# Making the first pair's operands of a feed-forward inside the last attention slots, and reordering a kernel's first loads

## The reference, cut to what matters

```python
x = layernorm(x + autocorrelation_attention(x))   # top lag 0 dominates on these data
sim = softmax(einsum("ncs,nds->ncd", ctx, x) * 256 ** -0.5, axis=1)
x = layernorm(x + einsum("ncd,nds->ncs", sim, ctx))
x = layernorm(x + x @ W_base.T + moe_lora(x, gate_W, A, B))   # 8 experts, rank 8, top 2
```

## Time and profile before

| | |
|---|---|
| three timed runs | 1957.73, 1959.69, 1960.36 us |
| median | 1959.69 us |
| the profiled execution | 1960.41 us |
| its span, first to last instruction | 1958.6 us |
| mean granted TensorE clock | 0.971 of full |
| busy: PE, DVE, ACT, POOL | 1783.3, 1362.4, 792.3, 171.4 us |
| DMA | 472.70 MB, mean 241 GB/s |

### The profile page before, as it was taken

How to read it: one execution, slowest core, us unless ns; L and a number is a source line. 1 busy time by engine, 2 the same in 40 slices (tenths; PEclk the granted TensorE clock), 3 DMA queues, 4 the chain that set the end, 5 groups by cost and what they waited for, 6 DMA issues and landing times. The chain is left out here.

```text
span 1958.6 us, 27039 instructions
## 1 busy us (share of the span) xinstructions
PE 1783.3 (91%) x10210; PEld 952.3 (49%) x10210; DVE 1362.4 (70%) x2607; ACT 792.3 (40%) x939; POOL 171.4 (9%) x362
## 2 busy tenths in 40 slices
PE   3899999999944969999999999998899999999997
PEld 2666666666621434445444445443344444444443
DVE  3888888888859866777666777689655565465553
ACT  5788888888745212222222212133222222122211
POOL 1212121212100000000000000000010010001000
PEclk8999999999976979999999999999999999999999
DMA  8799999999768499999999999955989988988883
GB/s 280 188 292 267 282 257 296 263 289 252 229 197 241 124 233 250 267 251 235 259 258 252 248 231 232 223 167 161 283 249 257 272 235 256 258 259 228 262 251 118
DMA packets 565595, 472.70 MB, mean 241 GB/s; under 512 B 498448, under 2 KB 502544, under 8 KB 544656
## 3 DMA queue, kind: packets, MB, share of 16 engines
q1 hardware_dynamic: 565456, 470.87, 87.7%
HBM read 237.51 MB, written 109.58 MB: 177 GB/s over the span
## 5 line engine op out<-in xcount | busy, mean ns | idle before, releaser
L1585 PE MATMUL bank_f<-w_hi_f,a_cols_f 128*128 128x512 f16 x3584 | 1091.9, 382 | 79.0 <-DMA a_cols_f<-rows_f 58.7
L1585 PE MATMUL bank_f<-w_lo_f,a_cols_f 128*128 128x512 f16 x1792 | 684.4, 382 | 0.0
L1585 PEld LDWEIGHTS bank_f<-w_hi_f,a_cols_f 128*128 128x128 f16 x3584 | 352.5, 98 | 509.3 <-DVE w_lo_f L1312 40.1
L1164 ACT ACTIVATE rows_f<-xn_f 128x1024 f16<-128x1024 f32 x78 | 82.4, 1057 | 497.7 <-DMA xn_f<-x_scratch 339.5
L1585 PEld LDWEIGHTS bank_f<-w_lo_f,a_cols_f 128*128 128x128 f16 x1792 | 176.2, 98 | 204.5 <-issue 4.0
L1343 DVE SCALAR_TENSOR_TENSOR y_f<-bank_f,w_iscale_f,y_f 128x512 f32<-128x512 f32 x192 | 134.6, 743 | 169.2 <-PE bank_f L1585 169.1
L656 PE MATMUL ps_s_fast<-k_both_fast,q_hi_fast 128*128 128x256 f16 x1024 | 171.2, 275 | 8.0 <-DMA k_both_fast<-v_lo_fast 7.0
L1343 DVE SCALAR_TENSOR_TENSOR y_f<-bank_f,w_iscale,y_f 128x512 f32<-128x512 f32 x192 | 134.9, 744 | 45.3 <-PE bank_f L1585 37.3
L1304 DVE TENSOR_TENSOR rows_f<-xn_f,rows_f 128x1024 f16<-128x1024 f32 x78 | 94.4, 1210 | 92.3 <-ACT rows_f L1164 92.3
L1304 DVE TENSOR_TENSOR rows_f<-sums_f,rows_f 128x1024 f16<-128x1024 f32 x63 | 76.9, 1221 | 112.5 <-ACT rows_f L1164 112.4
L1164 ACT ACTIVATE rows_f<-sums_f 128x1024 f16<-128x1024 f32 x63 | 66.3, 1053 | 199.3 <-DMA a_cols_f<-rows_f 196.9
(11 more groups left out here) (215 smaller groups left out, 2288.4 us busy)
## 6 DMA issues: line engine op xcount, KB each, us to landing
xbuf_fast<-x SPq DMA_DIRECT2D x32, 1024.0 KB, 7.9
x_scratch<-x2buf_fast SPq DMA_DIRECT2D x32, 1024.0 KB, 5.5
y_f<-x_scratch SPq DMA_DIRECT2D x32, 1024.0 KB, 8.0
xn_f<-x_scratch SPq DMA_DIRECT2D x62, 512.0 KB, 4.8
kept_scratch<-a_cols_f SPq DMA_DIRECT2D x45, 512.0 KB, 3.4
xn<-x_scratch SPq DMA_DIRECT2D x45, 512.0 KB, 6.7
a_cols_f<-kept_scratch SPq DMA_DIRECT2D x45, 512.0 KB, 9.0
cbuf<-ctx_in SPq DMA_DIRECT2D x16, 1024.0 KB, 5.5
```

What stands on the lines that cost most here:

```text
L1164: nc.scalar.activation(rows[g % 2][:, 0], source(i), ACT.Copy).then_inc(a_hi, 1)
L1585: ins = nc.tensor.matmul(bank[i][:], a_cols[:, i, part + kk, :], ww[:, W_SLOT[i], kk, :], start=(kk == 0 and part == 0 and ww is w_hi), st ...
```

## The change

1. **First loads.** In slot -2 SP issues context 0 and x 0, then the four key transposes of batch 0, with context 1 behind each of the last two, and only then x 1 and the tables. Weight tiles 0 and 1 are loaded for slots 1 and 2 instead of 0 and 1. DVE does both `value_low` of batch 0 before `x_stats(1)`.
2. **Pair 0's items in the attention.** `a_cols` becomes a buffer of the whole program. In the attention, `q_lo`, `q_hi`, the table `inv` and the two halves of x2's second tile live in it, until the items overwrite them. x2's rows 128 to 255 are loaded at the end of slot 12, rows 0 to 127 into `cbuf[0]` in slot 13. In slot 14 POOL makes the five sums and differences (`first_sum`), ACT the seven high parts (`first_high`), DVE the seven low parts (`first_lows`), in buffers that are free by then: `k_both[0]`, `v_hi[0]`, `v_lo[0]`, `xn0`, `xbuf[0]`. In slot 15 SP turns them (`turn_first`), between the two stores of batch 14. The prefetch of x2's first rows goes.
3. **Feed-forward.** Slot 0 makes no items and loads no blocks; the eight units follow one another. `wait_slot` doesn't wait in slot 0. Item numbers start with pair 1. The scratch of the squares of `ag_in` moves to `rows[1]`.
4. The two sets of `stored` semaphores become one, with a base for the pass that these data don't take, and `w_reduced` becomes a count of `w_summed`.

The diff, cut to its core:

```diff
+        a_cols = consts["a_cols"]
+        q_lo, q_hi = [two_items(i).rearrange("p (k c) -> p k c", c=C) for i in (2, 4)]
+        first_tile = two_items(0).bitcast(F32)
+        freed = nb % 2
+        f_rows = [k_free[:, i * L:(i + 1) * L] for i in range(4)] + [v_hi[freed][:, 0], v_hi[freed][:, 1], v_lo[freed][:, 0]]
+        SUM_ORDER, HIGH_ORDER = (3, 2, 4, 5, 6), (0, 1, 3, 2, 4, 5, 6)
...
+                def load_first(r):
+                    sp.wait_ge(stored[0][r], 16 * (base + 1))
+                    if r == 0:
+                        sp.wait_ge(vlo_done, R * (nb - 1) + 1)
+                        sp.dma_start(cbuf[0][:], x2_out[0:P, :]).then_inc(c_loaded[0], 16)
+                    else:
+                        sp.dma_start(first_tile, x2_out[P:2 * P, :]).then_inc(f_loaded, 16)
+
+                def turn_first(i):
+                    sp.wait_ge(f_lo, max(i + 1, 2))
+                    if i < 2:
+                        sp.wait_ge(f_sum, len(SUM_ORDER))
+                    elif i < NM - 1:
+                        sp.wait_ge(sim_done, R * nb)
+                        sp.wait_ge(folded, R * nb)
+                    else:
+                        sp.wait_ge(inv_done, R * nb)
+                    sp.dma_start_transpose(a_cols[:, i], f_rows[i]).then_inc(f_turned, 16)
+
                 def slot(n, half, parity):
+                    if n == nb - 1:
+                        store(n - 1, 1 - parity, (0,))
+                        for i in range(NM):
+                            turn_first(i)
+                        store(n - 1, 1 - parity, (1,))
+                        return
                     if isinstance(n, int) and n == -2:
                         for r in range(R):
                             load_context(0, r)
                         load_x(0, 0)
+                        for r in range(R):
+                            transpose_keys(0, 0, 0, r)
+                        for r in range(R):
+                            transpose_keys(0, 0, 1, r)
+                            load_context(1, r)
                         load_x(1, 1)
-                        load_weights(0)
                         sp.dma_start(fwd[:], consts["fwd_dram"]).then_inc(tables_loaded, 16)
                         sp.dma_start(inv[:], consts["inv_dram"]).then_inc(tables_loaded, 16)
+                        return
...
-                sp.dma_start(consts["xn0"][:], x2_out[0:P, :]).then_inc(prefetched, 16)
                 sp.wait_ge(fwd_done, 4 * nb)
-                sp.wait_ge(vlo_done, R * nb)
+                sp.wait_ge(f_lo, NM)
...
+                    def first_sum(i):
+                        one, two, op = OPERANDS[i]
+                        if i == 3:
+                            pool.wait_ge(f_loaded, 16)
+                            pool.wait_ge(w_squared, 2 * W_TILES)
+                            pool.wait_ge(p_ready, R * (nb - 1))
+                        elif i == 2:
+                            pool.wait_ge(c_loaded[0], 16 * (nb + 1))
+                        elif i == 4:
+                            pool.wait_ge(ctx_added, CG * (nb - 2) + NBANK)
+                        elif i == 6:
+                            pool.wait_ge(f_sum, 4)
+                        g.tensor_tensor(f_source[i], f_blocks[one], f_blocks[two], op).then_inc(f_sum, 1)
+
+                    if n == nb - 2:
+                        first_sum(SUM_ORDER[0])
                     if is_batch(n - 1, nb):
                         norm2(n - 1, 1 - parity, 1)
+                    if n == nb - 2:
+                        for i in SUM_ORDER[1:]:
+                            first_sum(i)
                     if cur and n < nb - 1:
                         norm2(n, parity, 0)
...
+                        nc.scalar.activation(f_parts[i][:, 0], f_source[i], ACT.Copy).then_inc(f_hi, 1)
...
+                        if j in (2, 3, 5, 6):
+                            first_highs((0, 1, None, 3, 2)[j - 2])
...
                     value_high(1)
+                    first_highs(4, 5)
                     softmax_exp(0)
+                    first_highs(6)
...
+                                v.tensor_tensor(f_parts[i][:, 1], f_source[i], f_parts[i][:, 0], ALU.subtract).then_inc(f_lo, 1)
...
+                    first_lows(0)
                     softmax_max(0)
...
                     softmax_norm(0)
+                    first_lows(1)
+                    first_lows(2)
                     softmax_max(1)
+                    first_lows(3, 4)
                     value_low(1)
                     softmax_norm(1)
+                    first_lows(5, 6)
...
                 wait_stored(sp, x2_stored, NP_)
-                load_block(0, A22)
-                load_block(0, A21)
                 load_unit(1)
                 load_unit(2)
-                turn(0, 0)
-                turn(0, 1)
-                load_unit(3)
...
                 for b in (A22, A21):
                     load_block(1, b)
+                load_unit(3)
+                load_b(0)
+                load_unit(4)
                 load_unit(5)
-                turn(0, 6)
-                load_b(0)
                 load_residual(0)
                 load_unit(6)
...
                 unit_high(0)
-                high_rows(0, 0)
-                high_rows(0, 1)
                 unit_high(1)
...
                 unit_low(0)
-                low_rows(0, 0)
-                combine(0, 2)
-                low_rows(0, 1)
                 unit_low(1)
```

More of the change, by code:

```diff
@@ L672, in slot @@
                             pe.wait_ge(w_summed, 4)
[L673 removed]
+                            nc.tensor.matmul(verdict_all, ones[:], verdict[:], start=True, stop=True).then_inc(w_summed, 1)
                         if j == CG - 1 and n != -1:
@@ L1942, in decoder_layer @@
         setup(nc, consts)
-        stored, stored_again = stored_sems("fast"), stored_sems("full")
-        attention_pass(nc, x, ctx_in, x2, w_chunks, b_rows, ag_in, consts, stored, EPS4_AT, "fast")
+        stored = stored_sems("x2")
+        attention_pass(nc, x, ctx_in, x2, w_chunks, b_rows, ag_in, consts, stored, 0, EPS4_AT, "fast")
         some_row_needs_it = nc.values_load(flag[0:1, 0:1], min_val=0, max_val=1)
@@ L1948, in decoder_layer @@
             autocorrelation(nc, x, z, forward_dram, inverse_dram, consts, stored)
-            attention_pass(nc, z, ctx_in, x2, w_chunks, b_rows, ag_in, consts, stored_again, EPS_AT, "full")
-            x2_in_place(nc, stored_again, nb)
+            attention_pass(nc, z, ctx_in, x2, w_chunks, b_rows, ag_in, consts, stored, 1, EPS_AT, "full")
+            x2_in_place(nc, stored, 2 * nb)
         feed_forward(nc, x2, out, w_chunks, b_rows, consts, stored)
```

124 lines of the change are left out of this document (71 added, 53 removed).

## The result

The changed kernel takes 1941.35 us, the median of 4 runs (1940.64 to 1942.99); the kernel before took 1959.12 beside it (4 runs). The ratio is 0.9906, 95% interval 0.9895 to 0.9918: faster by 17.8 us. A later repetition gave 1943.12 (4 runs), ratio 0.9909 (0.9892 to 0.9926). The forecast was 1935.0, within 1929 to 1942. Of its 25.0 us some 18 came; the time lies 0.7 us inside the range, and the repetition's 1.1 us outside it. The profiled execution has a span of 1940.8 where the one before had 1958.6, and its own time is 1942.99.

A forecast was written before the change was run, and what follows sets the result against it. Attention was taken as bound near TensorE, the feed-forward's first slot by VectorE. Terms: -9.5 (start) + 2.5 (last attention slots) - 18.2 (slot 0) + 0.2 (half clock) = -25.0, giving 1935.0 us, range 1929 to 1942.

The forecast's parts named there:

- The start: First loads: keys arrive before TensorE is free, context energy at 39.4 instead of 48.89; -9.5 us, ends -11 and -4.
- should land by 42: First loads: the tables, 1.5 MB behind 2 MB of x, arrive by 42 and are needed at 45.9.
- So I let the shift pass whole: Attention slots: a steady beat of 32.48 us over 14 slots, so the gain at the front is kept in full.
- The last attention slots: Slots 14 and 15: added sums, copies, differences and seven transposes delay the attention's end by 2.5 us, ends 0 and +5.
- VectorE: 0, if their inputs are on time: Slots 14 and 15: seven differences (8.0 us) fit where VectorE waits around the softmax halves, cost 0.
- ahead of the norm2 queued behind it: 0: Slot 14, GpSimd: the first sum ends at 522.1, before norm2's input at 522.8, cost 0.
- The rival named the port: Last slots: GpSimd's norm2 and VectorE's folds hold each other up, exponential 2.0 late, attention's end +3.8; 1936.5 us, chance 0.18.
- a start that gains half: First loads: tables, x of batch 1 or second context tile late, only 4 us gained; 1940.5 us, chance 0.08.
- Slot 0: Feed-forward's first slot: without items and waits VectorE's last weight unit ends at 640.6 instead of 658.8; -18.2 us.
- stays at 1.2 GHz: Feed-forward slot 0: TensorE, fed in bursts, needs 9.0 us a unit, gain 2.5 instead of 18; 1950.5 us, chance 0.05.
- They shift whole and gain nothing: Feed-forward slots 1 and 2: they start from unit 7's end on three engines, so they move earlier without further gain.
- SyncE: Slot 15: seven transposes might take 7.63 us each on the queue, decided from 6.1; 1970 us, chance 0.02.

The follow-up runs named there:

- brows_late: Changed kernel with the b_rows tile loaded and squared one slot later still; first addition of slot 0 at 57.48 us, one execution took 4997 us.
- guard_swap: Changed kernel with guard_lags reading its lag-0 value from PSUM as first operand and the maximum as scalar; 1942.20 us.
- low1_early: Changed kernel with item 1's difference made right behind the first, ahead of the softmax's maximum; 1941.17 us.
- both: Changed kernel with guard_lags reading PSUM first and item 1's difference made right behind the first; 1937.68 us.
- both_brows_sum6: Changed kernel with guard_lags from PSUM, item 1's difference early, b_rows a slot later, and item 6's sum on VectorE; 1934.67 us, ratio 0.9870.
- start_only: Kernel before with only the change's first slot: order of loads and key transposes, both v_lo back to back, b_rows one slot later; 1950.35 us.
- three_turns: Changed kernel with guard_lags from PSUM and the transposes of items 2 to 5 left out (wrong products, time only); 1933.28 us.
- brows_again: Second run of the changed kernel with the b_rows tile loaded and squared one slot later still; 1941.24 us.
- both_sum6: Changed kernel with guard_lags from PSUM, item 1's difference early and item 6's sum on VectorE, b_rows as in the change; 1936.64 us, ratio 0.9877.

## Why the prediction was right, and where it was off

**The start: right, and variable.** Predicted 9.5, measured 9.1 at slot 0. Each step held: keys there before TensorE (32.70), the energy at 38.82 where 39.4 was said, the logits at full clock. The tables landed at 46.7, against "should land by 42", and TensorE waited 1.15 us for them. The wait for `b_rows` was missed, but most of it is hidden (brows_late). What I did not see is that this gain differs from execution to execution. Stretch 54 to 58 of guard_swap and of low1_early:

```profile
54.00:58.00 4.00, 3.78 (x16) 2.07 (x16) 2.29 (x5) 4.00 (x8) 0.96 (x2) 0.61 1.01 236
```

```profile
54.00:58.00 4.00, 3.95 (x23) 2.15 (x22) 2.10 (x6) 3.80 (x6) 0.61 (x2) 1.00 1.01 225
```

TensorE's clock there is 1.00, the 2.4 GHz level, in the profiled executions of the changed kernel, its repetition, low1_early, both, brows_late and both_brows_sum6, whose first addition lies between 56.9 and 57.9. It is 0.57 to 0.74, partly the 1.2 GHz level, in start_only, guard_swap, three_turns, brows_again and both_sum6, where the first addition lies between 58.5 and 60.0. The stretch stands right behind TensorE's wait for ScalarE, but the length of this wait doesn't part the two groups: 1.8 to 3.1 us in the first, 2.3 to 3.3 in the second. What decides it stays open. So the lead at slot 0 is 8.8 to 9.8 us or 6.6 to 8.2, by the execution.

**"So I let the shift pass whole": right** up to slot 14 (8.6 of 9.1) and, in start_only, to the feed-forward.

**The last attention slots: the late transfers were seen, their size was not.** This term was +2.5 with ends 0 and +5, and measured +8.6, outside its ends. The prediction's own sign for it failed: VectorE's first weight unit was to start at 567.2 and started at 573.82. The steps, in the order in which they add up. The forecast puts the transfers' end at 573.7 - 9.5 = 564.2; they ended at 571.1, 6.9 later.
The lead was 8.6 instead of 9.5: 0.9.
The step that failed is "VectorE: 0, if their inputs are on time", and with it "ahead of the norm2 queued behind it: 0" for GpSimd. I timed the first sum and the three behind the first tile's banks, and never placed the second, which follows norm2 of batch 13 directly. Nor did I look, in VectorE's loop over the banks, for an instruction with two SBUF inputs. `guard_lags` is one, twice in each slot, and a sum met it both times: 3.9 us, where I had +0.7 for the exponential. That is 3.2 more. guard_swap shows that this was the cause, by the beat of 30.54 us. The duration itself was right: 2.35 us for 2.28.
The rival named the port, and put it at norm2 and the folds. In the changed kernel that place was free (norm2 at 528.91, its steps 0.18 to 0.55), only because the stall had pushed the folds behind it. In guard_swap it happened as described, with the exponential 1.6 us late where the rival had 2.0.
The seven transposes took 18.1 us instead of 17.4: 0.7. The 2.48 was near (9.61 for four, 2.40 each); a wait of 0.4 and a last one of 2.96 came on top.
The 4.8 MB behind them took 14.6 us instead of 12.5: 2.1. I had taken 416 GB/s; at a share of 1.01 it was 372, and the end of the last transpose still ran beside the first of them.
The sum is 6.9, of which the first 0.9 belongs to the lead. 4.1 us of it are lateness of the first transpose.
That 1941.35 lies within the range is in part luck. The upper end, 1942, was set for a start that gains half, which didn't happen; it had room for a loss in the last slots that no end of this term covered.

**Why neither edit alone gave anything back.** The prediction treated the transfers as a tail of fixed length behind one starting point. There are two starts: items 0 and 1 wait for a difference, items 2 to 5 for batch 15's logits.

**Slot 0: right.** Predicted 66.4 us of VectorE from the first unit to the last and no wait of over 1 us; measured 66.9 (573.82 to 640.75). 18.2 was forecast and 18.1 came, 0.3 of it by VectorE's earlier start (573.82 for 574.16). The granted clock was 0.90 over 591 to 624, most of it the 2.4 GHz level. It was 0.57 at 606 to 609, near the 1.2 GHz level, after TensorE had waited 3.2 us, until 604.6, for the router's weights; it fell again (0.78 over 624 to 627) while TensorE had no matmul. Rival "stays at 1.2 GHz" falls.

**"They shift whole and gain nothing": nearly.** The load of `xn` in slot 1 came 16.9 earlier, in slot 3 14.7, the end 17.8. The whole feed-forward is 1367.0 long where it was 1384.9, and 1364.3 to 1369.2 over the variants. Its own spread of 5 us is larger than what this part of the forecast was meant to resolve. I can't say what makes it.

**SyncE: right that it would not be slow** (2.4 us an item, where the rival needed 6.1).

## What to carry to other kernels

When long GpSimd instructions are put into a loop, list every instruction of VectorE in that stretch that reads two tensors from SBUF, the smallest too: a 0.22 us operation costs what is left of the sum, and reading one of the two tensors from PSUM removed the wait here. When transposes and copies are put in front of a barrier, add up the whole queue and find every event that may start a part of it, since moving one start alone gave nothing here until the next was moved as well. A gain at the front and a cost at the end can cancel at the barrier and hide each other, as the equal starts of the feed-forward did, so state each term at the barrier too, and take each away by itself once.

## What the runs showed of the hardware

**The stall is decided by where the operands lie, not by their size.** The same operation on one value per partition takes 2.02 us behind a sum with both tensors in SBUF, and 0.22 in guard_swap with one in PSUM and the other SBUF value as the per-partition scalar. The 128x512 additions of L598, which read PSUM, one SBUF tensor and a scalar, took 0.73 to 0.75 us beside the sums. "SBUF — State Buffer" of the Trainium skill (Who interferes with whom) says that an instruction of VectorE with two SBUF inputs and one of GpSimd that reads SBUF exclude each other, and that the later of the two waits for the whole of the other. The trace agrees both ways: L580 ends with the sum (517.88 and 517.87), and in guard_swap norm2's 530.41 + 0.70 = 531.11 ends with VectorE's difference (529.85 + 1.21 = 531.06).

**A 128x1024 f32 sum on GpSimd takes 2.35 us**, in all five, against 1.22 on VectorE. The estimate of 2.3 us from the Trainium skill's "GPSIMD Engine Reference" (Elementwise — side-by-side cycle accounting) agrees, and so does the 2.28 that I took from the rows; the lower end that I kept was too low.

**A transpose fills the queue like a copy of nearly twice its size here.** Between 540 and 554 the transposes moved 198 to 219 GB/s at a share of 1.06 to 1.16; between 558 and 571 copies moved 372 at 1.01. An item of 0.5 MB takes 2.4 us. "Advanced Engine Details and Errata" of the Trainium skill (X-Bar Transpose) expects 350 to 400 GB/s, about as much as a plain copy. By that the seven would take some 10 us, as an estimate; they took 18.1. The measurement decides, for items that lie in SBUF on both sides.

**The feed-forward starts 1.5 to 3 us after the last transfer; what holds it until then is open.** In the changed kernel the transfers are over at 571.1 and ScalarE starts at 573.76, in the kernel before, too, only after the last transfer. Part of it is the kernel's own wait: SyncE, ScalarE and VectorE wait there for every store of x2, batch 15's too (`wait_stored`), and these stores stand last on the queue. In three_turns and both_sum6 the profile names a store of x2 as what ended ScalarE's wait (8.35 and 10.43 us). But VectorE's first instruction of the feed-forward stands ahead of this wait in its program and is hardly earlier, 573.59 in the changed kernel. There is one more candidate in the traces: some 0.05 MB of instructions move through the DMA engines between 570.5 and 571.5 in the changed kernel, together with the last of the data, and between 564.5 and 565.5 in three_turns; VectorE starts 2 to 3 us later in both. Whether these instructions wait behind the data, or the end of the block waits for the data first, no run here separates.
